# A five-part kernel: a second layer with rings of four and centred weights, and a gate whose normalisation moves to ScalarE

## The reference

```python
# second layer, per image: 16 Fourier modes along each of the two axes,
# a complex 128x128 channel product per mode, back again, sum of both axes
h = xx + xy
h = relu(h @ ff_w0 + ff_b0) @ ff_w1 + ff_b1
mu = mean(h); var = mean((h - mu)**2)            # over the 128 channels
out = x + (h - mu) * rsqrt(var + 1e-5) * ln_g + ln_b
# last layer, its end: y has 256 channels per position
y = layernorm(y) * ln_w + ln_b                   # over the 256 channels
out = x + (y * silu(z)) @ W_out.T
```

## Time and profile before

| what | us |
|---|---|
| median of 3 runs (lowest to highest) | 18965.46 (18960.36 to 18978.39) |
| the profiled execution, its own time | 19011.53 |
| its span, first to last instruction | 19009.7 |
| second layer in it (loads to statistics) | about 3103 to 4441 |
| gate in it (first sum to the end) | about 18539 to 19010 |

### The profile page before, as it was taken

The page is one execution under the profiler, slowest core; times in us unless marked ns, Lnnn a source line. Parts: engine busy times, 40 slices in busy tenths (PEclk is TensorE's granted clock), DMA queues, the critical chain, the costliest instruction groups (busy, mean ns, idle before and its releaser), DMA issues. The chain is left out here.

```text
span 19009.7 us, 305966 instructions
## 1 busy us (share of the span) xinstructions
PE 15321.3 (81%) x109890; PEld 11063.0 (58%) x109890; DVE 16268.6 (86%) x20757; ACT 14205.6 (75%) x28037; POOL 12301.6 (65%) x8425
## 2 busy tenths in 40 slices
PE   8999999894222287888888888888888888888886
PEld 5666666571000036667666766666666676666663
DVE  6777774537777798999999999999999999999999
ACT  5666664323222258999999999999999999999994
POOL 1111110003444308999999999999999999999986
PEclk9999997877555699999999999999999999999998
DMA  1000000101111133333333333333333333343336
GB/s 58 15 13 15 13 16 32 59 21 49 35 35 35 41 147 137 124 122 116 123 120 133 134 127 133 135 126 126 122 117 124 118 125 133 126 135 134 126 115 213
DMA packets 829779, 1819.06 MB, mean 96 GB/s; under 512 B 205968, under 2 KB 436848, under 8 KB 822512
## 3 DMA queue, kind: packets, MB, share of 16 engines
q1 hardware_dynamic: 828272, 1799.49, 28.3%
HBM read 1522.41 MB, written 276.82 MB: 95 GB/s over the span
## 5 line engine op out<-in xcount | busy, mean ns | idle before, releaser
L1705 DVE TENSOR_TENSOR_SCAN sc_h<-ps,sc_dBu 128x512 f32<-128x512 f32 x8192 | 9442.3, 1203 | 419.3 <-ACT ps L1572 397.5
L1676 POOL TENSOR_TENSOR sc_dBu<-sc_du,sc_Bb 128x2048 f32<-128x2048 f32 x2048 | 9311.5, 4547 | 8.1 <-DMA sc_Bb<-BD 6.4
L1572 ACT ACTIVATE ps<-sc_de,sc_A 128x512 f32<-128x512 f32 x8192 | 5917.7, 771 | 205.4 <-DVE sc_h L1705 194.6
L1539 PE MATMUL ps<-base,sc_h 128*128 128x128 f32 x32768 | 4636.2, 281 | 1494.5 <-DVE sc_h L1705 647.0
L1637 ACT ACTIVATE sc_hs<-ps,sc_CT 128x256 f32<-128x256 f32 x12288 | 5160.5, 550 | 163.0 <-PE ps L1539 123.3
L1539 PEld LDWEIGHTS ps<-base,sc_h 128*128 128x128 f32 x32768 | 3588.1, 142 | 2573.3 <-DVE sc_h L1705 2241.8
L1551 PE MATMUL ps<-base,sc_hs 128*128 128x128 f32 x32768 | 4344.4, 276 | 0.8 <-ACT sc_Yd L1644 0.4
L1551 PEld LDWEIGHTS ps<-base,sc_hs 128*128 128x128 f32 x32768 | 3704.8, 142 | 602.3 <-issue 496.4
L449 DVE CUSTOM_DVE_ANT_0 l_T<-ps,l_rel 128x512 f32<-128x512 f32 x2048 | 1328.7, 686 | 840.8 <-PE ps L357 840.8
L302 POOL TENSOR_SCALAR l_nm<-l_mx 128x1 f32<-128x1 f32 x1024 | 270.7, 279 | 2531.6 <-DVE l_mx L449 2531.6
L416 ACT ACTIVATE l_P<-l_T,l_nm 128x1024 f32<-128x1024 f32 x1024 | 1177.0, 1149 | 319.6 <-POOL l_nm L302 319.6
(11 more groups left out here) (239 smaller groups left out, 18255.5 us busy)
## 6 DMA issues: line engine op xcount, KB each, us to landing
sc_Bb<-BD SPq DMA_DIRECT2D x2048, 512.0 KB, 6.2
sc_u<-U SPq DMA_DIRECT2D x256, 512.0 KB, 4.6
Y<-sc_Yt SPq DMA_DIRECT2D x256, 512.0 KB, 3.3
U<-cv_u SPq DMA_DIRECT2D x32, 2048.0 KB, 12.7
sc_Yt<-Y SPq DMA_DIRECT2D x128, 512.0 KB, 8.7
gt_y<-Y SPq DMA_DIRECT2D x128, 512.0 KB, 5.3
l_raw<-in_x SPq DMA_DIRECT2D x72, 288.0 KB, 4.3
st_x<-in_x SPq DMA_DIRECT2D x8, 2048.0 KB, 15.5
```

The source lines that it names most:

```text
L1539: t = nc.tensor.transpose(hT[g][:, j, h * 128:(h + 1) * 128], h_[:, h, k * 128:(k + 1) * 128], d["ident"])
L1572: nc.scalar.activation(dA[q % 3], de[n % 2][:, h, s0 * SL:(s0 + 1) * SL], ACT.Exp, scale=par[pno(n) % 2][3][:, h, m:m + 1]).then_inc(ex_do ...
L1676: nc.gpsimd.tensor_tensor(dBu[x % 3], du[n % 2][:, :, s0 * SL:(s0 + 1) * SL].unsqueeze(1).broadcast_to([128, 2, 2, SL]), Bb[x % NBB].unsqu ...
L1705: nc.vector.tensor_tensor_scan(hr[P % 3][:, x % 2, h, ::step], dA[(2 * x + h) % 3][:, ::step], dBu[P % 3][:, x % 2, h, ::step], 0.0, ALU.m ...
```

## The change

In the second layer:

- the weights `w0`, `w1` have buffers of their own and are loaded at the start. VectorE subtracts from each row of `w1` its mean over the outputs, and the bias likewise, so the second matmul gives `h - mu` at once: the mean matmul of `f3`, its subtraction and one copy are gone. `f3` is now the variance matmul; ScalarE writes `h - mu` and its square straight from PSUM, and the root takes EPS as its bias;
- VectorE's end of a tile is the reciprocal, two instructions with a scalar and two tensors, and the statistics; GpSimd does nothing in this layer;
- `XT`, `gT` and their banks are rings of four, and the multiplication of group `g-2` stands behind the turn of group `g`;
- the feed-forward buffers lie over `W`, `F` and `Gm` instead of `xn`: the next image is loaded behind the second forward part and normalised in steps 16, 20, 24 and 28 of the feed-forward part of the image before.

In the gate `nr` is four ScalarE instructions, Identity with scale `1/root` and bias `-mean/root`; VectorE makes that bias by one more small instruction in `sq`.

```diff
 def l1_steps():
...
+        if s >= 16 and s % 4 == 0 and s < 32:
+            order.append(("xn", s // 4 - 4))
...
-        XT, gT = ph.bufs(2, "xt", 4, 128), ph.bufs(2, "gt", 4, 128, parts=32)
+        XT = ph.bufs(4, "xt", 4, 128)
+        gT = [t[0:32] for t in XT]
...
+        h1r = [Wf[:, 2048 * i:2048 * i + 2048].rearrange("p (a b) -> p a b", a=4) for i in range(2)]
+        ddr, sqr, sdr, yr = over(Fl, 0, 4), over(Fl, 2048, 2), over(Fl, 3072, 3), over(Fl, 4608, 2)
+        xr, outr = over(Gf, 0, 4), over(Gf, 2048, 3)
+        tb, gb, hb, vb = [[bank[i] for i in r] for r in ((0, 1, 4, 5), (6, 7, 2, 3), (0, 1, 2, 7), (5, 6))]
...
+                e.dma_start(w0, I["ff0"]).then_inc(c_ld, 16)
+                e.dma_start(w1.rearrange("p a b -> p (a b)"), I["ff1"]).then_inc(c_ld, 16)
...
+                    if b + 1 < B:
+                        load_x(b + 1)
...
-                    nc.gpsimd.tensor_tensor(outr[N % 3], yr[N % 2], xr[N % 4], ALU.add).then_inc(add, 1)
...
+                        for g in range(32 + LAG):
+                            if g < 32:
...
+                                if g < 4:
+                                    pe.wait_ge(i_ev, 32 * idx)
+                                    if dr == 0 and b:
+                                        pe.wait_ge(h1a, 96 * b)
+                                        pe.wait_ge(h1v, 32 * b)
+                                        pe.wait_ge(sd_done, 32 * b)
...
+                            if g >= LAG:
+                                forward(idx, g - LAG)
...
-                        elif f in ("f3", "f4"):
...
+                        elif f == "f3":
+                            pe.wait_ge(h2_ev, 2 * N + 2)
+                            pe.wait_ge(sd_done, N - 1)
+                            nc.tensor.matmul(vb[n % 2], d["avg"], sqr[N % 2], start=True, stop=True).then_inc(v_mm, 1)
...
+                            nc.scalar.activation(ddr[N % 4], bank[3 + n % 2], ACT.Identity,
+                                                 bias=sm[:, 8:9]).then_inc(h2_ev, 1)
+                            act.wait_ge(v_mm, N - 1)
+                            nc.scalar.activation(sqr[N % 2], bank[3 + n % 2], ACT.Square,
+                                                 bias=sm[:, 8:9]).then_inc(h2_ev, 1)
...
+                            nc.scalar.activation(sdr[N % 3], vb[n % 2], ACT.Sqrt, bias=sm[:, 9:10]).then_inc(sd_done, 1)
...
                             nc.vector.reciprocal(s, s).then_inc(st, 1)
...
+                            nc.vector.scalar_tensor_tensor(out=y, in0=ddr[N % 4], scalar=sm[:, 5:6], in1=s, op0=ALU.mult,
+                                                           op1=ALU.mult).then_inc(y_dv, 1)
...
+                            nc.vector.scalar_tensor_tensor(out=outr[N % 3], in0=y, scalar=sm[:, 6:7], in1=xr[N % 4],
+                                                           op0=ALU.add, op1=ALU.add).then_inc(y_dv, 1)
...
 def gate(nc, pool, ps, d, I, xin, xout):
...
+                    elif kind == "nr":
+                        k, i = divmod(n, GR)
+                        act.wait_ge(rc, 2 * k + 2)
+                        y = yr[n % NY]
+                        for a in range(4):
+                            at = 4 * i + a
+                            t = nc.scalar.activation(y[:, a, :], y[:, a, :], ACT.Identity, bias=mvr[k % 3][:, at, 0:1],
+                                                     scale=sdr[k % 3][:, at:at + 1])
+                        t.then_inc(nrm, 1)
...
-                            t = nc.vector.tensor_scalar(y[:, a, :], y[:, a, :], mvr[k % 3][:, at, 0:1],
-                                                        sdr[k % 3][:, at:at + 1], ALU.subtract, ALU.mult)
...
+                        nc.vector.scalar_tensor_tensor(out=m, in0=m, scalar=-1.0, in1=sdr[n % 3], op0=ALU.mult,
+                                                       op1=ALU.mult).then_inc(rc, 1)
```

More of the change, by code:

```diff
@@ L578, in _ @@
                 pe = Eng(e)
+                pe.wait_ge(c_ld, 80)
+                nc.tensor.matmul(bank[7][:, 0:1], d["avg"], sm[:, 4:5], start=True, stop=True).then_inc(cb_mm, 1)
                 def forward(idx, g):
                     G = 32 * idx + g
-                    pe.wait_ge(c_ld, 48)
                     pe.wait_ge(x_cp, G + 1)
@@ L605, in _ @@
                         idx = 2 * b + dr
[L606 to L622, removed]
+                        for g in range(32 + LAG):
+                            if g < 32:
+                                G = 32 * idx + g
+                                need = 4 * b + (4 if dr else g // 8 + 1)
+                                pe.wait_ge(xa, need)
+                                pe.wait_ge(xv, need)
+                                if g < 4:
[4 more added lines that the diff above has]
+                                        pe.wait_ge(sd_done, 32 * b)
+                                else:
+                                    pe.wait_ge(x_cp, G - 3)
+                                for j in range(4):
+                                    ln = 4 * g + j
+                                    t = nc.tensor.transpose(tb[g % 4][:, j * 128:(j + 1) * 128],
+                                                            xn[:, ln, :] if dr == 0 else xn[:, :, ln], d["ident"])
+                                t.then_inc(xt_mm, 1)
+                            if g >= LAG:
+                                forward(idx, g - LAG)
                         pe.wait_ge(w_ld, 16 * (idx + 1))
@@ L633, in _ @@
                         pe.wait_ge(gd, 8 * idx + 8)
[L634 to L642, removed]
+                        for g in range(32 + LAG):
+                            if g < 32:
+                                if g >= 4:
+                                    pe.wait_ge(gt_cp, 32 * idx + g - 3)
+                                for j in range(4):
+                                    t = nc.tensor.transpose(gb[g % 4][0:32, j * 128:(j + 1) * 128],
+                                                            Gm[:, 4 * g + j, :, :].rearrange("p a b -> p (a b)"), d["ident"])
+                                t.then_inc(gp_mm, 1)
+                            if g >= LAG:
+                                inverse(idx, g - LAG)
                     pe.wait_ge(i_ev, 64 * b + 64)
-                    pe.wait_ge(ff_ld, 32 * (b + 1))
+                    pe.wait_ge(cw, 5)
                     for f, n in steps:
@@ L677, in _, with normalise @@
                 act = Eng(e)
-                for b in range(B):
[L679 to L683, removed]
+                def normalise(b, q):
+                    act.wait_ge(x_ld[q], 16 * (b + 1))
+                    part = xf[:, q * 4096:q * 4096 + 2048]
+                    nc.scalar.activation(part, part, ACT.Identity, bias=d["nb"][:, b:b + 1],
+                                         scale=d["rs"][:, b:b + 1]).then_inc(xa, 1)
+                for q in range(4):
+                    normalise(0, q)
+                for b in range(B):
                     for dr in range(2):
@@ L693, in _ @@
                             act.wait_ge(gp_mm, 32 * idx)
+                            if b:
+                                act.wait_ge(y_dv, 64 * b)
+                                for i in range(3):
+                                    act.wait_ge(out_st[i], 16 * ((32 * b + 2 - i) // 3))
                             nc.scalar.copy(Gm[:, :, ky, :],
@@ L698, in _ @@
                             act.wait_ge(gp_mm, G + 1)
[L699 to L702, removed]
+                            act.wait_ge(d_mm, 32 * idx + 32)
+                            act.wait_ge(i_mm, G - 3)
+                            nc.scalar.copy(gT[g % 4].rearrange("p a b -> p (a b)"), gb[g % 4][0:32, :]).then_inc(gt_cp, 1)
+                    act.wait_ge(c_ld, 80)
+                    act.wait_ge(cw, 5)
+                    act.wait_ge(g_mm, 32 * b + 32)
+                    act.wait_ge(gp_mm, 64 * b + 64)
                     for f, n in steps:
@@ L708, in _ @@
                                 act.wait_ge(h2_mm, N - 1)
[L709 removed]
+                                nc.scalar.activation(h1r[N % 2][:, m, :], hb[m], ACT.Relu,
                                                      bias=sm[:, m:m + 1]).then_inc(h1a, 1)
@@ L746, in _ @@
                             v.wait_ge(gp_mm, 32 * idx)
+                            if b:
+                                for i in range(3):
+                                    v.wait_ge(out_st[i], 16 * ((32 * b + 2 - i) // 3))
                             nc.vector.tensor_copy(Gm[:, :, ky, :],
```

176 lines of the change are left out of this document (72 added, 104 removed).

## The result

The changed kernel takes 18672.56 us (median of four, 18662.65 to 18678.23), the kernel before in the same session 18971.92: a ratio of 0.9842, 95% interval 0.9825 to 0.9859, 299 us less where 208 were predicted. It lies 52 us under the forecast's own range (18725 to 18795) and 7 us under the one for eight cases in ten (18680 to 18840). The profiled execution took 18678.23 us. Against that of before, 19011.5, this is 333 us; where the other 34 come from is told with the first experiment.

What follows compares the result with a forecast made beforehand. TensorE was taken to bound the second layer's parts, VectorE the gate. Gains of 48.0 + 13.5 + 49.5 + 0 + 97 = 208 us, from runs at 18965.5, gave 18757 us; own range 18725 to 18795, eight in ten 18680 to 18840.

Steps and rivals of the forecast that it cites:

- Second layer, feed-forward: Feed-forward steps of both images: one matmul of ten per tile goes, 0.857 us less in each of 56 steps, 48.0 us.
- the drain: After the second image's last `f1`: VectorE ends the remaining tiles in 32.1 us instead of 45.6, gain 13.5 us.
- the change of image: Between the images: the next one lies normalised already, its product starts after 99.8 us instead of 149.3, gain 49.5 us.
- 1.63: Rival, feed-forward: VectorE's instructions with a scalar and two tensors take 1.63 us, costing 44 us, total 18801; chance 0.03.
- Rings of four. 0.: Second layer's rings: one wait of 0.23 us saved four times, offset by two weight loads, gain 0.
- The first rival: Inverse parts: with the wait gone all four stay at 2.4 GHz, 82 us faster, 18675; chance 0.12.
- The downward rival: Inverse parts: three turns in a row at the head lower the clock of all four, 82 us slower, 18839; chance 0.13.
- The gate: Last stage: L1872's work moves from VectorE to ScalarE, step 7.07 to 5.2 us, gain 97 us (39 to 117).

Runs made afterwards that it cites:

- the first experiment: The kernel before, unchanged, profiled once more: 19011.63 us, with the same two inverse parts at 92 us.
- gate_only: The kernel before with the changed gate alone (`nr`, `sq`, the turned mean): 18890.83 us in the profile, 120.8 less; ratio 0.9933.
- warm: The changed kernel with useless dense matmuls ahead of two forward parts and the waits at each part's head taken group by group: 18661.27 us, ratio 0.9829.
- rings_only: The kernel before with only four buffers and four banks for each ring and a lag of two: 18859.46 us in the profile, 152.2 less; ratio 0.9929.
- the finer waits: The changed kernel with only the waits at each part's head taken group by group: 18635.08 us, ratio 0.9829; run once more, 18651.81 us, ratio 0.9826.

## Why the prediction was wrong

- **Second layer, feed-forward; the drain; the change of image: right.** From the first `f1` of an image to the product of the next it was 409.5 us and is 336.3, 73.2 less (24.0 + 49.5 predicted); in the second image, to the last statistics, 305.76 became 268.29, 37.5 less (24 + 13.5). VectorE's new instructions took 0.75 us each, close to the 0.69 taken and not 1.63.
- **"Rings of four. 0.": the step that failed.** It priced waits, and the only wait was 0.23 us. What it removed was the low clock of parts that TensorE bounds: 40.2 + 40.0 us for two inverse parts, 31.7 for a forward part, 4 for products and heads, 116 in all. The prediction had the first two as a rival at 0.12, though its trace showed the clue: same instructions, two clocks, and a wait a few us before the clock falls. The downward rival did not come: with three turns in a row at the head none of 36 inverse parts fell. The sentence of the Trainium skill behind it (TensorE: Matmul & The Clock Gate, "Part 4: PE-mode transpose"), that a turn "doesn't count as PE-busy the same way", did not decide here: inverse parts of 51 us and forward ones of 47, a third turns each, ran at 2.4 GHz.
- **The gate: mechanism right, size off.** ScalarE's work was put at 3.06 + 4 x 0.54 = 5.2 us. The 3.06 were taken where its pairs stood alone; in a row they take 1.32 + 1.14, and the root with its table loads 0.35, 2.8; four scalings take 1.97, not 2.16. That adds up to 4.78, and with GpSimd relieved the step was 4.70. With GpSimd's 4.73 beside it the step is 4.85: 117.6 us less for the 53 steps and 4.9 for the tail, where 97 were predicted. The reading of the earlier trace rows holds for all of L1872: in the profile of before 98 of its 256 instructions last over 1.5 us, and each of them ends 0.15 us after an instruction of GpSimd; no short one lies within one. The Trainium skill's advice to leave arithmetic to VectorE (ScalarE: Activation LUTs, "Rules for kernel authors") would have cost the 121 us that `gate_only` shows.
- **Terms against.** The parts begin 4.2 us later behind the weight loads (predicted 0). 12 us are lost in the convolution before the scan, 531.8 us before and 544.1 after. Its matmuls in both, the kernel before first:
```profile
6604.00:7107.00 503.00, 468.75 (x1059) 197.02 (x1059) 441.00 (x373) 273.79 (x266) 1.06 (x6) 0.97 0.38 151
```
```profile
6381.00:6896.00 515.00, 475.31 (x1058) 199.87 (x1059) 440.40 (x373) 273.88 (x266) 1.06 (x6) 0.95 0.37 148
```
The clock is low there for 20.5 us before and 41.0 after. Part of it varies with nothing changed: the convolution takes 529.4 to 535.2 us in the six profiles of kernels that keep the second layer's old feed-forward part. But it takes 543.7 to 545.1 in eight of the nine that have the new one (536.0 in `warm`), so most of the loss goes with the change, in a stage whose code it doesn't touch. How, no run shows.
- **The sum.** 208 + 116 + 26 (gate) - 4 - 12 = 334, against 333 between the profiles. The first session's medians differ by 299, one inverse part less, since by their times the runs of before had one low part where the profile had two. The first rival's condition came true, all four inverse parts at 2.4 GHz. That its 18675 comes near the result of 18672.56 is luck all the same: it took 82 us off a median that held only one low part, and had neither the forward part nor the gate's 26 nor the terms against.
- **The range.** It was said to hold one inverse part either way. Such a part is 41 us, and from 18757 the range reaches 32 down and 38 up.

## What to carry to other kernels

Where TensorE bounds a part and its granted clock is not the same in parts with the same instructions, the head of such a part is to be priced as the clock: rings of four with a lag of two, whose only wait to save was one of 0.23 us, were worth 152 us in `rings_only`, and nothing with a lag of one. Take ScalarE's cost from start to start in a full row, not from the lengths of instructions that stand alone. Before a profile's distance from the median is carried along as a constant, see whether the executions lie in steps.

## What was not expected of the hardware

- One program's executions differ in steps of the size of a whole part at the other clock: 40 us, an inverse part, between clusters from 18928 to 19022 us.
- A part that is two thirds small matmuls and one third turns runs at either level: 80 or 48 us forward, 92 or 52 inverse. The first direction's forward part, behind an idle TensorE, ran at 1.2 GHz in every profile but for its start: it was at 2.4 for some 2 us behind the dense matmuls (`warm`, first image), and in the changed kernel's second image for the 8 us ahead of its wait for VectorE.
- GpSimd's sums did not slow down beside ScalarE's scalings (2.36 us each, 2.39 before), while VectorE's scaling beside GpSimd took 2.43 instead of 0.40.
- Why a forward part stays low in one kernel, image or execution and not in another is not known. None of the three slow executions of the finer waits was profiled, so what is low in them stays open.
